# The last tile's transposed context comes whole from memory; weight scans are spread and eight of them moved; 80 rows are loaded in place of 128

## The reference, cut to what matters

```python
x = x + _L0_xattn_ref(_layernorm(x), ctx_2048, ctx_2048, conv_w, conv_b, bn_gamma, bn_beta)
    # energy = x1 @ ctx^T; attn = softmax(energy, -1); attn /= 1e-9 + attn.sum(axis=1)
    # x_r = attn @ ctx; t = x1 - (conv_w @ x_r + conv_b)
    # x1 + relu(batch norm of t, mean and variance over all items and all 1024 columns)
x = x + _L0_attn_ref(_layernorm(x), Wq, Wk, Wv, Wo, lambdas, g)   # differential attention, 8 heads
x = x + _L0_ffn_ref(_layernorm(x), W1, b1, W2, b2)                # W1, W2 made ternary first
    # ternarize: delta = 0.05 * max|W|, alpha = mean of |W| over |W| > delta, W -> alpha * sign(W) * mask
```

## Time and profile before

| | us |
|---|---|
| median of 3 runs | 1380.77 |
| lowest, highest | 1377.85, 1381.84 |
| the profiled execution | 1379.24 |
| its span | 1377.4 |
| PE busy | 1334.1 (97% of the span) |
| DVE busy | 878.7 (64%) |
| ACT busy | 495.1 (36%) |
| cross attention, to the end of PE's last weighted sum | about 0 to 485 |
| value projection on PE | 497 to 614 |
| output projection on PE, with the last head | 842 to 960 |

### The profile page before, as it was taken

How to read it: one execution, slowest core, us unless ns; L and a number is a source line. 1 busy time by engine, 2 the same in 40 slices (tenths; PEclk the granted TensorE clock), 3 DMA queues, 4 the chain that set the end, 5 groups by cost and what they waited for, 6 DMA issues and landing times.

```text
span 1377.4 us, 17833 instructions
## 1 busy us (share of the span) xinstructions
PE 1334.1 (97%) x6850; PEld 651.2 (47%) x6850; DVE 878.7 (64%) x1484; ACT 495.1 (36%) x765; POOL 2.4 (0%) x10
## 2 busy tenths in 40 slices
PE   7999999999999979999999999999999999999994
PEld 4554646444454434444555555444444444444442
DVE  3232424324242288888889996755999997777974
ACT  1121302113021122116877775112545455544432
POOL 0000000000000000000000000000000000000000
PEclk9999999999999989999999999999999999999998
DMA  9999999999999587845565669341487775222264
GB/s 379 419 421 420 421 422 420 422 421 421 417 398 393 234 321 255 315 168 164 161 182 154 172 174 339 107 168 52 167 271 226 242 264 196 77 77 77 77 180 152
DMA packets 141044, 356.25 MB, mean 259 GB/s; under 512 B 63008, under 2 KB 89760, under 8 KB 115360
## 3 DMA queue, kind: packets, MB, share of 16 engines
q1 hardware_dynamic: 137792, 343.56, 68.5%
q10 hardware_dynamic: 3168, 11.54, 2.1%
HBM read 308.40 MB, written 46.66 MB: 258 GB/s over the span
## 4 chain that ended last, share of the span: by engine, by line
PE 74%; issue 14%; DMA 6%; DVE 4%; ACT 1%; DVEq 0%; POOLq 0%; POOL 0%
PE ps L1048 13%; PE ps L1153 13%; PE ps L1309 9%; PE ps L1220 8%; PE ps L962 7%; PE ps L1269 6%; PE ps L1107 5%; PE ps L1000 4%; DMA ctxT<-in_ctxT 3%; PE ps L979 2%; PE ps L1030 2%; PE ps L982 2%; DMA w_scan<-in_w2t 1%; PE ps L1173 1%; DMA x_t<-in_x 1%
## 5 line engine op out<-in xcount | busy, mean ns | idle before, releaser
L1358 PE MATMUL ps<-t_half,hl 128*128 128x512 f16 x896 | 193.6, 379 | 0.0
L1048 PE MATMUL ps<-ctx_sb,attnT 128*64 128x512 f32 (+1 forms) x832 | 180.3, 593 | 0.0
L699 ACT ACTIVATE stg<-ps 128x512 f32<-128x512 f32 (+1 forms) x80 | 44.4, 555 | 345.5 <-PE ps L979 173.4
L1358 PEld LDWEIGHTS ps<-t_half,hl 128*128 128x128 f16 x896 | 87.7, 98 | 105.7
L962 PE MATMUL ps<-ctxT,x1T 128*64 128x512 f32 x512 | 115.8, 596 | 1.8 <-DMA ctxT<-in_ctxT 1.8
L872 ACT ACTIVATE hl<-hb,al 128x512 f16<-128x512 f32 x112 | 79.2, 720 | 97.4 <-PE ps L1358 83.7
L1048 PEld LDWEIGHTS ps<-ctx_sb,attnT 128*64 128x64 f32 (+1 forms) x832 | 58.9, 137 | 115.4 <-issue 108.0
L1862 DVE SCALAR_TENSOR_TENSOR hl<-hb,al,hl 128x512 f16<-128x512 f32 x112 | 81.9, 749 | 48.7 <-ACT hl L872 48.5
L1107 PE MATMUL ps<-wv_sb,x2T 128*128 128x512 f32 x256 | 112.0, 596 | 0.0
L1220 PE MATMUL ps<-wo_sb,oT 128*128 128x512 f32 x256 | 111.6, 593 | 0.3 <-ACT oT L778 0.3
L1456 DVE COPY stg<-ps 128x512 f32<-128x512 f32 (+1 forms) x80 | 50.9, 639 | 82.2 <-PE ps L982 43.0
(11 more groups left out here) (220 smaller groups left out, 1810.5 us busy)
## 6 DMA issues: line engine op xcount, KB each, us to landing
ctxT<-in_ctxT SPq DMA_DIRECT2D x64, 1024.0 KB, 22.4
ctx_sb<-in_ctx SPq DMA_DIRECT2D x40, 1024.0 KB, 17.3
ctx_sb<-in_ctx SPq DMA_DIRECT2D x8, 4096.0 KB, 28.3
ctx_sb<-in_ctx SPq DMA_DIRECT2D x16, 2048.0 KB, 32.5
w_scan<-in_w1t SPq DMA_DIRECT2D x32, 512.0 KB, 6.4
w_buf<-in_w1t SPq DMA_DIRECT2D x32, 512.0 KB, 4.1
w_scan<-in_w2t SPq DMA_DIRECT2D x32, 512.0 KB, 5.5
w_buf<-in_w2t SPq DMA_DIRECT2D x32, 512.0 KB, 4.7
```

Source lines behind the costliest of these rows:

```text
L1048: ins = mm(bank(ea + hf)[C * b:C * b + C, :], attnT[0:w, slots[mt], C * b:C * b + C], ctx_sb[0:w, mt, b, hf * BANK:hf * BANK + BANK], star ...
L1358: ins = mm(bank(b), hl[:, r % RING, n, s * P:s * P + P], t_half[:, r % BRING, :], start=(fresh and k == 0 and n == 0), stop=(k == HK - 1 a ...
```

## The change

Five things are changed.

1. **Tile 7 has no transposes out of its natural context.** The host passes two more forms: `ctxW` (row blocks 8 to 11 transposed, for all tiles; each of its four parts per tile is two chunks of 512 columns, 1024 KB) and `ctxE` (block 12 of tile 7 transposed, two halves of 260 KB). For tile 7 parts 0 and 1 go through the `ctxT` ring behind the chunks, parts 2 and 3 into `stg` and the two halves into places of `x_t` and `x1T` (`load_apart`, behind a wait until the last energies of tile 6 are done). PE multiplies straight from there (`loaded_energies`, `tail_energies`). ACT and DVE have no copies to make for this tile.
2. **The natural form of tile 7 is loaded later and in another order**: groups 5, 7, 0, 1, 2, 6, 3, 4, each still behind its `pv_done`, so that all wait for group 5, which tile 6 is done with only after five others.
3. **Row block 12 is loaded with 80 rows (TAIL_ROWS) in place of 128**, for all eight tiles. 65 of them are used.
4. **The loads between the blocks are cut differently**: `tok` tiles 0 and 1, `xo` tiles 0 and 1, `wv_sb`, then `tok` 2 to 6 and `xo` 2 to 7. ACT's `relu(2)` moves behind the copies of the first transposes, with a wait for the second part of `tok`.
5. **Scans**: 40 in the value projection in place of 48. `V_SCANS` gives 2, 6, 7, 7, 7, 7 for tiles 2 to 7, a third of them ahead of `both(t)`, a third behind it and a third between the variance and its root, and 4 behind tile 7. The output projection has 24: four ahead of `normal(8)` and four at each of tiles 0 to 4.

```diff
+TAIL_ROWS = TAIL + (-TAIL) % 16
+LOADED = (0,) * (NT - 2) + (0, NC)
+def pairs(p):
+    if p < BY_ROW:
+        return SINGLES
+    return [("wide", c) for c in range(LOADED[p], NC)] + (SINGLES[-2:] if p < NT - 1 else [])
+def slots_of_tile(p):
+    ring = [(p, "chunk", c) for c in range(NC)] + [(p, "wide", i) for i in range(min(LOADED[p] // 2, 2))]
+    return ring if p < NT - 1 else ring + [(p, "apart", i) for i in range(2)]
-SCANS_V = 48
+SCANS_V = 40
+V_SCANS = (0, 0, 2, 6, 7, 7, 7, 7, 4)
...
+            def load_apart():
+                sp.wait_ge(e_done, first_pair(NT - 1))
+                for i in range(2):
+                    sp.dma_start(slot((NT - 1, "apart", i)), ctxW_in[NT - 1, 2 + i]).then_inc(apart_got, 16)
+                for i in range(2):
+                    sp.dma_start(tails[i][:, :, :, :], ctxE_in[i]).then_inc(apart_got, 16)
             def load_N(q, g):
                 m0, m1 = N_GROUPS[g][0], N_GROUPS[g][-1] + 1
+                if m1 == MT:
+                    sp.dma_start(ctx_sb[0:TAIL_ROWS, m0, :, :], ctx[q, m0 * P:m0 * P + TAIL_ROWS]).then_inc(ctx_in[g], 16)
+                    return
...
                     load_T(p + 1, range(7, NC))
+                    load_T(p + 1, range(min(LOADED[p + 1] // 2, 2)), "wide")
+                    if p + 1 == NT - 1:
+                        load_apart()
+                        next_N((5, 7, 0, 1, 2, 6, 3, 4))
+                        break
                     next_N(range(0, 5))
...
-            sp.wait_ge(ctxT_used, NC * NT)
+            sp.wait_ge(ctxT_used, len(USES))
             sp.wait_ge(n_stored, 16 * (NT - 1))
-            sp.dma_start(tok[:, 0:NT - 1, :], n_dram[0:NT - 1].rearrange("t p n -> p t n")).then_inc(n_in, 16)
+            load_tok(0, 2)
             sp.wait_ge(pv_done, G * NT - 7)
-            for i in range(2):
-                h4 = slice(4 * i, 4 * i + 4)
-                sp.dma_start(xo[:, h4, :], x_v[h4].rearrange("t p n -> p t n")).then_inc(s_in[i], 16)
+            load_xo(0, 2, s_in[0])
             sp.wait_ge(pv_done, G * NT - 3)
             sp.dma_start(wv_sb[:, :, :], wv.rearrange("(c p) n -> p c n", p=P)).then_inc(wv_in, 16)
+            load_tok(2, NT - 1)
+            load_xo(2, NT, s_in[1])
...
+            def loaded_energies(p):
+                wides = [u for u in slots_of_tile(p) if u[1] != "chunk"]
+                for j, use in enumerate(wides):
+                    if use[1] == "apart":
+                        pe.wait_ge(apart_got, 64)
+                    else:
+                        k = RING_NO[use]
+                        pe.wait_ge(ctxT_got[k % SLOTS], 16 * (k // SLOTS) + 16)
+                    for i in range(2):
+                        c = 2 * j + i
+                        for b in range(2):
+                            ins = mm(bank(2)[C * b:C * b + C, :], x1T[:, p % 2, c, C * b:C * b + C], halves(use)[:, i, b, :],
+                                     start=(c == 0), stop=(c == NC - 1))
+                    ins.then_inc(ctxT_used, 1)
+            def tail_energies(p):
+                for c in range(NC):
+                    for b in range(2):
+                        ins = mm(bank(3, TAIL)[C * b:C * b + C, :], x1T[:, p % 2, c, C * b:C * b + C],
+                                 tails[c // 4][:, c % 4, b, :], start=(c == 0), stop=(c == NC - 1))
+                ins.then_inc(e_done, 1)
...
+            for t in range(2, NT):
+                n = V_SCANS[t]
+                next_scans((n + 1) // 3)
+                both(t)
+                next_scans((n + 2) // 3)
+                norm2(t, n // 3)
+            next_scans(V_SCANS[NT])
...
-            for _ in range(2):
+            for _ in range(4):
                 scan(n_scan, w_scan2)
                 n_scan += 1
             normal(H)
...
-                for _ in range(3 if t else 2):
+                for _ in range(4):
```

More of the change, by code:

```diff
@@ L384, in width, with slot, halves, used_by @@
             return P if mt < MT - 1 else TAIL
+        def slot(use):
+            return ctxT[:, RING_NO[use] % SLOTS, :, :] if use[1] != "apart" else stg[:, 2 * use[2]:2 * use[2] + 2, :, :]
+        def halves(use):
+            return slot(use) if use[1] == "apart" else slot(use).rearrange("p c (b m) -> p c b m", b=2)
+        def used_by(p):
+            return USE_NO[p, "chunk", NC - 1] + 1
         def unit_slots(units):
@@ L451, in _ @@
                 if p + 2 < NT:
-                    load_T(p + 2, range(0, 4 if p < 2 else 2))
+                    load_T(p + 2, range(0, 4 if p < 2 or LOADED[p + 1] else 2))
                 next_N(range(5, 6))
-                if p >= 2 and p + 2 < NT:
+                if p >= 2 and p + 2 < NT and not LOADED[p + 1]:
                     load_T(p + 2, range(2, 4))
@@ L741, in _ @@
                       ACT.Copy).then_inc(x2_out, 1)
+                if t == 0:
+                    act.wait_ge(n_in, 32)
+                    relu(2)
                 act.wait_ge(xs_ready, t + 1)
@@ L968, in pair_transposes @@
                 n = pair_no(p, e)
-                for g in [e // 2] if e % 2 == 0 and (p < BY_ROW or e == 8) else range(4) if e == 0 else []:
+                for g in [e // 2] if e % 2 == 0 and p < BY_ROW else range(4) if e == 0 else [4] if e == len(pairs(p)) - 2 else []:
                     pe.wait_ge(ctx_in[g], 16 * p + 16)
@@ L1008, in later_pairs @@
             def later_pairs(p):
-                for e in range(4, E, 2):
+                n = len(pairs(p))
+                for e in range(4, n, 2):
                     two(pair_transposes, p, e)
@@ L1013, in later_pairs @@
                     put_x1T(p + 1)
-                two(pair_energies, p, E - 2)
+                two(pair_energies, p, n - 2)
             def weights_T(p):
@@ L1075, in _ @@
                 weigh_ctx(p)
-                if p + 1 < NT:
+                if p + 1 < NT and LOADED[p + 1]:
+                    chunk_energies(p + 1, range(4, NC))
+                    if p == 5:
+                        loaded_energies(6)
+                        two(pair_transposes, 6, 0)
+                        two(pair_transposes, 6, 2)
+                        two(pair_energies, 6, 0)
+                        later_pairs(6)
+                    else:
+                        loaded_energies(7)
+                        tail_energies(7)
+                elif p + 1 < NT:
                     chunk_energies(p + 1, range(4, NC - 1))
@@ L1529, in row_stats, with next_scans, norm2 @@
                 V.tensor_scalar(rs[:, 0, 0:1], mv2[:, 1:2], EPS, None, ALU.add).then_inc(var_ready, 1)
-            def norm2(t):
+            def next_scans(n):
+                for _ in range(n):
+                    scan(scanned_tiles[0], w_scan)
+                    scanned_tiles[0] += 1
+                    if scanned_tiles[0] == WT:
+                        V.wait_ge(scanned, WT)
+                        V.tensor_reduce(wpk[:, 0:1], wmx[:, 0, :], AX.X, ALU.max).then_inc(wmax_ready, 1)
+            def norm2(t, scans=0):
                 if t:
@@ L1535, in norm2 @@
                 row_stats(xo[:, t, :], None if t else 0)
+                next_scans(scans)
                 V.wait_ge(root_ready, NT + 2 + t)
```

96 lines of the change are left out of this document (52 added, 44 removed).

## The result

| | before | after |
|---|---|---|
| median of 5 runs, us | 1379.56 | 1388.45 |
| lowest, highest | 1377.85, 1381.84 | 1383.78, 1390.84 |
| span of the profiled execution | 1377.4 | 1386.7 |

A forecast was written before the change was run, and what follows sets the result against it. PE, busy for 97% of the span, was taken as the bound, so gains must shorten its work or waits. 8.70 + 0.96 + 1.45 = 11.1 us off a median of 1380.77 gave 1369.7; range 1366 to 1375.5, own range 1367 to 1372.

The forecast's parts named there:

- 80 rows for 128: Block 12's loads: 384 KB less per tile shortens chunk waits at tiles 1 and 4, 0.96 + 1.45 = 2.4 us, or 0.
- the short transfers save no time: Rival, chance 0.14: block 12's 80-row loads gain nothing, leaving 8.7 us of gain, 1372.1 us.
- the rule that I cited against this part: Trainium skill on block 12's loads: 128 partitions and 1 MiB or more for most bandwidth; sum 8.7 us, not 11.1.
- The transposes of tile 7: PE at tile 7: four groups of 1.89 us and a short one of 1.14 us come off in full, 8.70 us.
- What is loaded for it: Tile 7's transposed context, 4616 KB: 11.5 us of DMA, landed by about 421, over 13 us before PE wants it.
- the natural form: Tile 7's weighted sum: 12,928 KB land by 453.4, with 17 us of cover; any rate above 270 GB/s would do.
- The clock: PE's granted clock after tile 7's idle 3.35 us: kept as is, 0, with -1.5 and +1.5 us as bounds.
- the sum of 12.6 us: Total gain if, by the skill's rule that transposes are not activity, taking out tile 7's transposes favours the full clock.
- The loads between the blocks: Before the value projection: hidden; tile 2 ready at 500.5, wanted at 508.0, cover 7.5 us, wait under 321 GB/s.
- the scans: DVE's scans, 1.15 us each, in value and output projections: all put at 0.
- The rival of a late tile 2: Rival, chance 0.08: value projection's tile 2 comes late at 248 GB/s; half of 10 us gives 1374.8, all 1379.8.
- The output projection's DVE: Rival, chance 0.06: the output projection's eight scans come to the path, 9.2 us, 1378.9 us.

The follow-up runs named there:

- experiment 1: The changed kernel with row block 12 loaded with 128 rows again, all else kept: 1370.13 us, ratio 0.9928 to the kernel before.
- the one with even places: The changed kernel with block 12 of tiles 1 to 7 loaded as 64 rows into every second partition, whole for tile 0: 1366.53 us, ratio 0.991.
- experiment 3: The kernel before with parts 1 and 2 alone (tile 7), block 12 with 128 rows, loads and scans as before: 1374.87 us, ratio 0.9962.
- experiment 2: The kernel before with one edit alone, row block 12 loaded with 80 rows: 1401.22 us, ratio 1.0142.
- the kernel with the old scans: The changed kernel with 128 rows and the scans as before, the loads between the blocks cut the new way: 1383.92 us, ratio 1.0025.
- the runs with 64 rows: The changed kernel with 64 rows of block 12 for tiles 1 to 7: 1380.61 us; into every second partition 1366.53; from every second source row 1380.96.
- the run of 80 + 48 rows: The changed kernel with block 12 in two transfers, rows 0 to 79 and rows 80 to 127 behind them: 1401.64 us, ratio 1.0162.

## Why the prediction was wrong, step by step

**The step that failed is "80 rows for 128".** It was put at 2.4 us of gain, with nothing as its other end, and it measured 18.3 us of loss. Both bounds came from transfers that reach all 128 partitions, and I wrote myself that no row had another kind. The reason for taking the upper end, that packets of 8 KB per row are paid by their bytes, does not hold for these: the packets themselves become slower, those of neighbours too. For 128 partitions one half of the term was seen. With 640 KB in place of 1024 the wait at tile 4's chunks is gone, and they take 7.09 us without a break where before they took 8.54, just the 1.45 us of the sum. The other half, 0.96 us at tile 1, no run tests: in that kernel tile 0's block, which it rests on, is loaded whole.

```profile
221.36 7.09 PE L1029 MATMUL ps<-ctxT,x1T 128*64 128x512 f32 x32
```

A third bound was in order, that such a transfer slows the queue it lies in. What stood in its place: seven slow stretches of 7 to 14 us at half the rate, 13.9 us more of waits for the context, and 4.1 us at the half clock behind two of them. My rival for it, "the short transfers save no time", stopped at nothing. And the rule that I cited against this part speaks of the same thing. I gave it 0.14 and let it change only 2.4 us.

**The transposes of tile 7**: 8.70 us forecast, the weighted sum comes 8.78 us earlier in experiment 1. Right, though not that closely: it is 9.36 us within the tile, since the energies, put at what they cost before, also became about 0.7 us shorter.

**What is loaded for it, and the natural form**: hidden as forecast; after has no wait for `ctxT`, `stg` or `ctx_sb` in tile 7, even with the slower queue. Right.

**The clock** at tile 7 was put at 0, with 1.5 us either way. The bounds were right, and the value is a matter of the single execution. Behind the same idle 3.35 us the turned weights take one of three times in the 15 traces: 3.1 us in three of them, 4.5 to 4.8 us in seven (before 4.63, after 4.53, experiment 1 4.75) and 5.9 to 6.0 us in five. Rows of the kernel before with parts 4 and 5, of the one with even places, of experiment 3 and of experiment 2:

```profile
457.65 3.14 PE L1040 MATMUL ps<-conv_s,prob 128*128 128x130 f32 x26 [3.35 <-DVE conv_s L1497]
```

```profile
446.23 3.14 PE L1121 MATMUL ps<-conv_s,prob 128*128 128x130 f32 x26 [3.35 <-DVE conv_s L1594]
```

```profile
447.67 5.90 PE L1115 MATMUL ps<-conv_s,prob 128*128 128x130 f32 x26 [3.35 <-DVE conv_s L1588]
```

```profile
477.71 5.97 PE L1033 MATMUL ps<-conv_s,prob 128*128 128x130 f32 x26 [3.36 <-DVE conv_s L1490]
```

The first and the last of these kernels have tile 7's transposes, the two between have not, so the traces do not bear out that taking them out favours the full clock, on which the sum of 12.6 us rested. What I had not forecast is the clock behind new waits: 2.6 us at tile 4 of after, 2.2 us behind the first wait in the kernel with the old scans.

**The loads between the blocks and the scans**, both put at nothing: right as a pair and wrong apart. Together on the kernel before they give 0.16% (1378.33 us). But part 1 without them keeps 5.6 us of its 8.7 (1374.87), and with them all of it (1370.13): they carry 4.7 us. The cover at tile 2 was 2.0 us, not 7.5: the 11.0 million bytes took from the issue of `wv_sb` at 469.18 to 500.38 us, 353 GB/s, not 410. The rival of a late tile 2 has its break at 321 GB/s, which is not far away.

**The output projection's DVE**: its eight scans cost nothing. From the last head's matmuls to the last transposes PE takes 90.32 us before (869.80 to 960.12) and 90.31 after (879.45 to 969.76).

**The sum** with the failed step left out was 8.7 us, and experiment 1 measured 10.3 us on the medians and 9.1 us on the spans. With 640 KB over 128 partitions, where the terms of 8.70 and 1.45 us apply, the first transposes of the value projection come at 483.20 us, 11.6 us earlier than the 494.84 of before, against a sum of 10.15; 0.7 us of this was there at the end of tile 1's chunks, before either term acts, and about 0.7 us are the shorter energies. The median, 1367.81, lies within the forecast's own range of 1367 to 1372. The row of PE's timeline:

```profile
483.20 1.97 PE L1200 MATMUL ps<-cst,x2s 128*128 128x128 f32 x8 [7.46 <-DVE x2s L1659]
```

That kernel leaves part of block 12 unread, as the runs with 64 rows do, so it isn't a version to use. The best that computes the reference is experiment 1, 1370.13 us, faster than both kernels. Block 12 with fewer rows spread over the partitions in a form that computes the reference wasn't tried.

**Open** is why the slow stretch lasts 7 to 14 us when the transfer itself moves 512 to 768 KB, and why two partial transfers that fill 128 rows are worse than one. The idea recorded with the run of 80 + 48 rows, that a partial transfer throws the engines out of a common spacing and a second one that brings each to eight rows restores it, forecast 1371 to 1378 us for that run; it took 1401.64. The rival recorded beside it, that a transfer collides only where its rows per engine don't fit, forecast 1367 to 1369 for 64 rows; they took 1380.61. Neither holds as it was put.

## What to carry to other kernels

Where DMA queues are full, a cut in a load's size should be made in the bytes per partition and not in the number of partitions: 128 rows of 5 KB took no longer than whole rows, 80 rows of 8 KB lost 18.3 us, with the same 640 KB per transfer. When no row of the trace shows the form of transfer that a change brings in, "nothing" is no bound for its cost; look at the DMA share beside the GB/s after the run, since full engines with fewer GB/s say at once that packets have become slower, and where in time. And a gain on the critical path must be followed to the next loads and DVE work: 3.1 of 8.7 us were lost there until the loads and the scans had been moved together.
